# A gated cross-attention layer with routed experts: a constant product behind every score block of the first quarter

## The reference

```
# stage 1: additive attention to 77 context tokens
f   = layernorm(x)
h   = tanh((ctx @ Ws)[:, None] + (f @ W)[:, :, None] + b)    # token x 77 x 256
rho = h . w                                                  # one score for each token and context token
att = softmax(rho + mask)
th  = att @ ctx
x   = x + tanh(g0) * (tanh(th . Wcw + bcw) * f + tanh(th . Wcb + bcb))
# stage 2: 8 experts, two for each token
n   = layernorm(x)
p   = softmax(n @ router.T); keep the two largest of 8
x   = x + tanh(g1) * sum over the two: p_e * (gelu(n @ w1[e].T) @ w2[e].T)
```

## Time and profile before

| | |
|---|---|
| time, median of 3 runs | 592.97 us (592.93 to 594.25) |
| the profiled execution's own time | 590.49 us |
| its span, first to last instruction | 588.7 us |
| mean granted TensorE clock | 0.944 |
| busy: PE, PEld | 523.3 us (89%), 338.6 us (58%) |
| busy: DVE, ACT, POOL | 359.1 us (61%), 354.4 us (60%), 119.2 us (20%) |
| chain that ended last | PE 60%, DVE 18%, ACT 10%, DMA 4%, issue 4%, SP's queue 3% |

### The profile page before, as it was taken

One profiled execution on the slowest core, in us unless ns is written; L12 is line 12 of the kernel. 1 busy time (PEld: TensorE's weight loads), 2 busy tenths in 40 slices (PEclk: granted clock), 3 DMA queues, 4 the chain that ended last, 5 costly groups with the idle time before them and its releaser, 6 DMA issues.

```text
span 588.7 us, 10199 instructions
## 1 busy us (share of the span) xinstructions
PE 523.3 (89%) x3432; PEld 338.6 (58%) x3433; DVE 359.1 (61%) x1190; ACT 354.4 (60%) x314; POOL 119.2 (20%) x96
## 2 busy tenths in 40 slices
PE   7887979665799898989899999999899999999994
PEld 5432323102255443545454555788799999999993
DVE  4889997898875799885799987376111111111110
ACT  1678999987998988999978999241011111111110
POOL 2000000050001253501243111136222222222222
PEclk9688989777899979999979999999999999999998
DMA  4101940055212026422128433349765555555541
GB/s 133 37 0 48 419 187 1 1 182 213 87 63 90 10 85 204 133 89 90 71 61 232 141 116 96 127 130 264 229 185 185 180 179 179 179 179 179 170 98 19
DMA packets 32937, 77.56 MB, mean 132 GB/s; under 512 B 4576, under 2 KB 25696, under 8 KB 26752
## 3 DMA queue, kind: packets, MB, share of 16 engines
q1 hardware_dynamic: 24848, 67.22, 33.1%
q0 software_dynamic: 7344, 9.72, 8.8%
q10 hardware_dynamic: 704, 0.09, 0.2%
HBM read 60.73 MB, written 16.29 MB: 131 GB/s over the span
## 4 chain that ended last, share of the span: by engine, by line
PE 60%; DVE 18%; ACT 10%; DMA 4%; issue 4%; SPq 3%; POOL 1%; POOLq 0%; DVEq 0%
PE h_ps L705 20%; PE y_bank L717 19%; PE rho L670 13%; DVE hbuf L872 8%; ACT hbuf L558 8%; PE misc L650 3%; DMA out<-x_res 2%; PE xsT_bank L659 2%; PE xsT_bank L693 1%; SPq L370 1%; SPq L371 1%; ACT hbuf L564 1%; PE h_ps L615 1%; DMA w_st<-in_w 1%; PE misc L641 1%
## 5 line engine op out<-in xcount | busy, mean ns | idle before, releaser
L558 ACT ACTIVATE hbuf<-hbuf 128x2048 f32<-128x2048 f32 (+2 forms) x160 | 247.3, 1594 | 38.8 <-DVE hbuf L872 38.4
L872 DVE TENSOR_SCALAR hbuf<-featT,txtb 128x512 f32<-128x512 f32 x525 | 216.2, 480 | 20.4 <-PE rho L670 19.2
L670 PE MATMUL rho<-hbuf,wpad 128*32 128x512 f32 x1232 | 175.0, 649 | 34.9 <-ACT hbuf L564 19.5
L705 PEld LDWEIGHTS h_ps<-xsT,w_st 128*128 128x128 f32 x1280 | 151.3, 194 | 28.3 <-issue 25.2
L705 PE MATMUL h_ps<-xsT,w_st 128*128 128x128 f32 x1280 | 157.4, 280 | 2.4 <-DMA w_st<-in_w 1.2
L717 PE MATMUL y_bank<-w_sb,hgT 128*128 x640 | 151.5, 387 | 2.3 <-DVE y_sb L1047 2.3
L717 PEld LDWEIGHTS y_bank<-w_sb,hgT 128*128 128x128 f32 x640 | 118.4, 192 | 38.3 <-issue 24.1
L587 ACT ACTIVATE hgT<-h_ps 128x1024 f32<-128x1024 f32 x40 | 40.8, 1019 | 165.5 <-PE h_ps L705 165.4
L511 POOL DMA_INDIRECT out<-y_sb,meta x40 | 69.0, 1726 | 300.4 <-DMA out<-y_sb,meta 126.9
L670 PEld LDWEIGHTS rho<-hbuf,wpad 128*32 128x32 f32 x1232 | 30.3, 113 | 121.2 <-ACT hbuf L564 46.2
L1033 DVE COPY xsT<-xsT_bank 128x256 f32<-128x256 f32 x40 | 16.9, 424 | 87.7 <-PE xsT_bank L693 87.7
(11 more groups left out here) (136 smaller groups left out, 189.7 us busy)
## 6 DMA issues: line engine op xcount, KB each, us to landing
w_st<-in_w SPq DMA_DIRECT2D x40, 1024.0 KB, 4.9
w_sb<-in_w SPq DMA_DIRECT2D x8, 1024.0 KB, 12.7
xs<-row_scratch SPq DMA_DIRECT2D x40, 132.5 KB, 4.5
row_scratch<-pad SPq DMA_DIRECT2D x33, 132.5 KB, 21.2
x_res<-in_x SPq DMA_DIRECT2D x4, 512.0 KB, 4.7
out<-x_res SPq DMA_DIRECT2D x4, 512.0 KB, 5.8
hgT<-in_x SPq DMA_DIRECT2D x3, 512.0 KB, 3.4
out<-y_sb,meta POOLq DMA_INDIRECT x40, 6.3
```

Of the source, the lines that this page charges most:

```text
L558: ins = s.activation(h, h, ACT.Tanh)
L670: ins = t.matmul(rho[q % 2][32 * j:32 * j + 32, :], wpad[:, c, 31 - r:63 - r], hbuf[:, k % HB, j, :], start=(k == 0), stop=(last and c == ...
L705: ins = t.matmul(h_ps[:, k * P:(k + 1) * P], w1_st[:, par, c, k * P:(k + 1) * P], xsT[:, c, :], start=(c == 0), stop=(c == DC - 1))
L872: ins = v.tensor_scalar(hbuf[:, k % HB, j:j + 1, :], featT[:, c, q:q + 1, :], txtb[:, c, bb, CG * r + j:CG * r + j + 1], None, ALU.add)
```

## The change

A function `idle_products` is added on PE. It multiplies the 128x128 constant tile `ones` (float32, all ones) by itself into the first 128 columns of the score bank that this quarter doesn't use, and nothing reads the result. It is called behind each block's preparation steps: two products for each of the 40 blocks of quarter 0, three for each of blocks 0 to 5 of quarter 1, and two for each of blocks 6 to 13 (114 products in all). As the other bank holds the projected context when quarter 0 begins, PE first waits until DVE has read it (`setup_sb`).

```
+        FIRST_TURN = TURN[0] - NBLK
...
+            def idle_products(q, n):
+
+                for _ in range(n):
+                    t.matmul(rho[(q + 1) % 2][:, 0:P], ones[:], ones[:], start=True, stop=True)
+
             def quarter(q):
                 e = None
                 if q:
                     settle("turn_scores", q - 1)
+                else:
+                    pe.wait_ge(setup_sb, DC)
                 for k in range(NBLK):
...
                     if q and k in PE_S:
                         settle(PE_S[k], q - 1)
+                    if q == 0 or (q == 1 and k < FIRST_TURN):
+                        idle_products(q, 3 if q and k < 6 else 2)
                     for name, i in todo:
```

## The result

The changed kernel took 603.65 us (median of 4 runs, 601.33 to 604.0) beside 593.61 us for the kernel before (4 runs, 592.93 to 594.92): a ratio of 1.0164, 95% interval 1.0142 to 1.0186. The change costs 10.0 us. The profiled execution took 601.33 us, its span is 599.6 us, and its mean granted clock rose from 0.944 to 0.961. So the clock is better and the time worse. (In after, PE's lines stand one later than before, and `sum_block`'s addition is L882, the score copy L897.)

What follows compares the result with a forecast made beforehand. PE was taken to be late only at four pile-ups of preparation steps in quarter 0, otherwise waiting for DVE and ACT. Delays 0.9 + 0.6 + 2.2 + 5.0 = +8.7 us on 592.97 gave 601.7 us, range 596.4 to 606.4.

Steps and rivals of the forecast that it cites:

- (a): Quarter 0, 18.2 to 30.0 us, up to the gate projections: +0.9 us, bounds -0.9 and +3.8.
- the middle case: At (a), the clock rises at the same moment as in the run before: +0.9 us on the gate projections.
- (b): Quarter 0, project0 at 33.99 to the block ending at 45.30: four pairs +2.2, held clock -1.6, net +0.6 us.
- (c): Quarter 0, project0 at 60.97 to the block ending at 70.64, already at full clock: four pairs, +2.2 us.
- (d): Quarter 0, project0 at 86.58 to the scores' end at 100.68, no PE gap: nine pairs, +5.0 us.
- The upper bound of the price: A pair, with the parting of two blocks, costs PE 0.495 to 0.57 us for each block; 0.55 taken.
- the delay passes on: After quarter 0's score copy, nothing takes up the +8.7 us on the way to the first routed tile.
- the 8.4 us: Quarter 1: what its 34 products, at 0.2475 us each, would cost if other engines' work did not hide them.
- Rival 1: Faster, the clock was the limit: gains in (a) and (b), pairs vanish in PE's waits, 588.8 us; chance 0.12.
- Rival 2: No change: busy PE has hidden room in (c) and (d), 7.2 us go, +1.5 stays: 594.5 us; chance 0.09.
- its weight-load share: Weight loads' busy share in (d), 5.03 of 14.10 us, 36%: by the skill page most PE room left, +1.5 or less.
- Rival 3: Slower still: clock isn't held, PE enters (c) and (d) late, 606 us or a little over; chance 0.08.

Runs made afterwards that it cites:

- four products: The changed kernel with four products instead of two behind each block of quarter 0, quarter 1 unchanged: 617.59 us, ratio 1.0445 against the kernel before.
- the pile-ups alone: The changed kernel with pairs only behind quarter 0's blocks 4 to 8, 17 to 21 and 30 to 39: 604.85 us, ratio 1.0209 against the kernel before.

## Why the prediction was right

The forecast was +8.7 us; measured were +10.0, and 603.65 us lies within the forecast's own range, 596.4 to 606.4. By its steps:

- (a) +0.9: the gate projections ended 12.8 us after block 0's start instead of 11.8, +1.0. The clock rose at about 27.6 us, as in the run before, which was the middle case. The first pair cost 1.05 us, not 0.9.
- (b) +0.6: 34.87 to 46.71 is 11.84 us against 11.31, +0.5. The clock held and project0 took 1.98 us.
- (c) +2.2: 62.87 to 74.68 is 11.81 us against 9.67, +2.1.
- (d) +5.0: 90.80 to 110.74 is 19.94 us against 14.10, +5.8. This term was too small. I took 0.55 us for a pair and block; six of the nine pairs stand between two blocks and cost 0.64 besides making each block 1.00 us, so 1.64 instead of 0.925, 0.715 for a pair. The upper bound of the price, 0.57, was exceeded; it left out what the product itself loses behind a block of 32-column tiles, where a pair takes 0.64 us instead of 0.45 behind a projection.
- The rest, 0.7 us of the 10.2 up to the score copy, lies between the places, where the sum had nothing. I had PE catching up with DVE behind them; at 1.64 us a block against DVE's 1.62 it hardly does, and DVE was held up behind more blocks, 13 times instead of 9. Of the 0.7, 0.5 come right behind (b), where DVE waited for one more block, up to 48.39 us.
- That the delay passes on held but for 0.3 us: +9.76 at the first tile. That quarter 1's products are hidden held in that the 8.4 us didn't come; a cost of up to about 2 us isn't excluded.

Some luck was in the sum. The chain of before goes over PE at a fifth place, just ahead of (c), in the stretch from 55.2 to 58.6 us that the prediction says hardly touches the path. Before, and then after:

```profile
54.94 1.76 PE misc L641 x8
56.70 1.91 PE rho L670 x8
```

```profile
56.84 1.31 PE misc L642 x8
```

In after PE has no gap from this turn to project0 at 62.87, and three pairs, 1.73 us, stand on the path. The clock, now high there, gave as much back: from the turn to project0 it is 6.03 us both times. The prediction had counted neither.

Rival 1, the clock as the limit, had a real part: (b), and the run with half the products away from the pile-ups, faster than before, fits it. But (d) had no waits to hide nine pairs in. Rival 2, hidden room on a busy PE, falls with the 2.1 and 5.8 us that (c) and (d) cost, and with the number of products: once PE had no gap, further products were paid. The Trainium skill ("Trainium Kernel Development and Optimization", Performance Expectations) speaks of how near a kernel is to its roofline, and names the weight loads' busy share as one of two good measures of it. Taken as the prediction took it, as the room left on PE, its weight-load share doesn't fit this stage: the share in (d) of after is 9.35 of 19.90 us, 47%, and in quarter 0 with four products 60.35 of 105.10, 57%, while DVE waits for PE's blocks in both, 13.1 and 26.5 us over quarter 0. Rival 3 didn't come about with 128 columns; with eight, the clock did stay low in quarter 1. What the prediction said for it, that the clock fell with PE busy most of the time just ahead, was misread: in the 3 us ahead of the low stretches at 34.8, 55.2 and 79.1 us of before PE was busy for 0.84, 1.33 and 1.07 us.

## What to carry to other kernels

Work that only holds the clock up is paid like any other wherever its engine is the late one: leave it out where preparation steps pile up, and try it in that engine's waits ahead of a low stretch that lies on the path. Here such places gained 3.3 us together, and none of them alone a gain that the time could show. A mean over the quarter (PE busy for 71.4 of 82.5 us before) hid that one stretch of 14.1 us had no room at all. A better granted clock in the profile isn't a better time.

## What the runs showed of the hardware

- A float32 product with a 128x128 weight tile cost only about a sixth less for 8 columns than for 128: a pair between two blocks took 0.54 and 0.64 us, and all of quarter 0's products 8.4 and 10.2 us.
- A busy PE is not always given the full clock: with eight-column products between the blocks, PE was busy for 24.5 of 24.5 us at 1.2 GHz.
- Full-width products between blocks of four 32-column tiles cost more than the two apart: 1.64 us for block and pair, against 0.925 and 0.495, 1.42 together, in streams of their own.
- The same code meets the clock differently: block 0 took 1.94 us in before and after, and 1.06 or 1.07 in others whose lists are the same up to there (pairs behind blocks 2 and 3, four products, the pile-ups alone). The profiled executions also differ by 2.5 us in what follows the last score block (214.3 to 216.8 us), where no run changes anything. A single gain of 1 to 2 us can't be read from one execution's time.
